# The start of a quantised feed-forward kernel: first two tiles by column block, other load queues, four part buffers

## The reference, cut to what matters

```python
scale = cond @ norm_w.T + 1.0                       # one row of 256 per sequence
ms = jnp.mean(x * x, axis=-1, keepdims=True)
h = x * (scale[:, None, :] * jax.lax.rsqrt(ms + EPS))
u = h @ up_w.T                                      # 256 -> 2048
val, gate = jnp.split(u, 2, axis=-1)
h = val * jax.nn.gelu(gate, approximate=False)      # 1024 wide
hq = act_quant(h)      # round(h * 127 / max|h|), per token
wq = weight_quant(down_w)   # -1, 0, 1 times the mean of |down_w|
y = hq @ wq.T + x                                   # 1024 -> 256
```

## Time and profile before

| | |
|---|---|
| median of three runs | 429.09 us |
| the profiled execution, own time | 429.27 us |
| its span, first to last instruction | 427.5 us |
| TensorE busy | 421.1 us (99%) |
| VectorE busy | 280.4 us (66%) |
| ScalarE busy | 186.4 us (44%) |
| GpSimd busy | 179.9 us (42%) |
| HBM read and written | 20.00 MB and 8.39 MB |

### The profile page before, as it was taken

One profiled execution on the slowest core, in us unless ns is written; L12 is line 12 of the kernel. 1 busy time (PEld: TensorE's weight loads), 2 busy tenths in 40 slices (PEclk: granted clock), 3 DMA queues, 4 the chain that ended last, 5 costly groups with the idle time before them and its releaser, 6 DMA issues.

```text
span 427.5 us, 7667 instructions
## 1 busy us (share of the span) xinstructions
PE 421.1 (99%) x2081; PEld 337.6 (79%) x2081; DVE 280.4 (66%) x539; ACT 186.4 (44%) x334; POOL 179.9 (42%) x323
## 2 busy tenths in 40 slices
PE   7999999999999999999999999999999999999997
PEld 5688888888887888887888888888878888878786
DVE  4987567556577566576565675565675665765676
ACT  5753444443444444444434444434444434444441
POOL 1564435435345344354344354353453353553520
PEclk9999999999999999999999999999999999999999
DMA  8434443334444334434244433343443344342324
GB/s 281 147 80 115 100 118 103 75 97 123 98 105 115 71 100 106 115 98 107 74 114 98 120 100 77 94 123 98 108 113 73 98 111 109 98 108 75 87 51 124
DMA packets 82024, 45.01 MB, mean 105 GB/s; under 512 B 68256, under 2 KB 68704, under 8 KB 81888
## 3 DMA queue, kind: packets, MB, share of 16 engines
q1 hardware_dynamic: 81584, 44.33, 39.8%
q10 hardware_dynamic: 432, 0.59, 0.4%
HBM read 20.00 MB, written 8.39 MB: 66 GB/s over the span
## 4 chain that ended last, share of the span: by engine, by line
PE 94%; DMA 1%; DVE 1%; SPq 1%; POOL 1%; issue 1%; ACT 0%; DVEq 0%; POOLq 0%
PE p_gate L678 41%; PE p_val L678 41%; PE p_y L698 12%; DMA up_raw<-up_w_t 1%; SPq L219 1%; DVE y_sb L500 0%; PE p_val L650 0%; POOL a_hi L311 0%; POOL scaled L308 0%; PE p_gate L650 0%; DVE q_rounded L526 0%; DVE h L547 0%; PE p_gate L657 0%; POOL a_lo L315 0%; DVE last_max L509 0%
## 5 line engine op out<-in xcount | busy, mean ns | idle before, releaser
L547 DVE SCALAR_TENSOR_TENSOR h<-p_val,rstd,gelu 128x512 f32<-128x512 f32 x128 | 95.3, 746 | 129.9 <-PE p_val L678 129.5
L389 ACT ACTIVATE gelu<-p_gate,rstd 128x512 f32<-128x512 f32 x128 | 87.5, 684 | 149.1 <-PE p_gate L678 139.4
L304 POOL TENSOR_TENSOR mean_sq_eps<-mean_sq,rms_eps 128x1 f32<-128x1 f32 x64 | 12.2, 190 | 224.3 <-PE p_val L678 210.3
L361 ACT ACTIVATE q<-q_rounded 128x1024 bf16<-128x1024 f32 x63 | 66.7, 1058 | 78.2 <-DVE q_rounded L582 78.2
L678 PE MATMUL p_gate<-up_hi,a_lo 128*128 128x512 f32 x248 | 80.6, 406 | 0.6 <-POOL a_lo L315 0.6
L678 PE MATMUL p_val<-up_hi,a_hi 128*128 128x512 f32 x248 | 78.2, 396 | 0.0
L678 PE MATMUL p_val<-up_hi,a_lo 128*128 128x512 f32 x248 | 78.1, 396 | 0.0
L678 PE MATMUL p_val<-up_lo,a_hi 128*128 128x512 f32 x248 | 78.1, 396 | 0.0
L678 PE MATMUL p_gate<-up_lo,a_hi 128*128 128x512 f32 x248 | 78.1, 395 | 0.0
L678 PE MATMUL p_gate<-up_hi,a_hi 128*128 128x512 f32 x248 | 78.1, 395 | 0.0
L568 DVE TENSOR_REDUCE h_max<-h 128x1 f32<-128x1024 f32 x63 | 76.6, 1216 | 1.2
(11 more groups left out here) (74 smaller groups left out, 247.1 us busy)
## 6 DMA issues: line engine op xcount, KB each, us to landing
xt_in<-x_t SPq DMA_DIRECT2D x32, 256.0 KB, 2.8
x_all<-x SPq DMA_DIRECT2D x32, 256.0 KB, 2.9
out<-y_sb SPq DMA_DIRECT2D x31, 256.0 KB, 2.0
up_raw<-up_w_t SPq DMA_DIRECT2D x6, 256.0 KB, 5.4
down_raw<-down_w_t SPq DMA_DIRECT2D x1, 1024.0 KB, 8.0
q_t<-q SPq DMA_TRANSPOSE x63, 3.1
up_raw<-up_w_t ACTq DMA_DIRECT2D x2, 256.0 KB, 3.1
out<-y_sb SPq DMA_DIRECT2D x1, 128.0 KB, 2.0
```

The lines of the kernel that those rows point to most:

```text
L304: pool.tensor_tensor(mean_sq_eps[:, j:j + 1], mean_sq[:, j:j + 1], rms_eps[:, :], ALU.add).then_inc(pool_step, 1)
L361: act.activation(q[j % 2][:, :], q_rounded[j % 2][:, :], ACT.Copy, bias=-ROUND).then_inc(q_ready, 1)
L389: act.activation(gelu[c][:, :], p_gate[c][:, :], ACT.Gelu, scale=rstd[:, j:j + 1]).then_inc(gelu_done, 1)
L547: nc.vector.scalar_tensor_tensor(h[s][:, c * W:(c + 1) * W], p_val[c][:, :], rstd[:, j:j + 1], gelu[c][:, :], op0=ALU.mult, op1=ALU.mult). ...
```

## The change

- The four pieces of tiles 0 and 1 run in another order: block 0 of tile 0, block 0 of tile 1, block 1 of tile 0, block 1 of tile 1 (`early_up`). Of these two tiles the gate and value of tile t go to p_gate[t] and p_val[t] instead of p_gate[c] and p_val[c]. Inside a column group of these tiles high and low products alternate.
- ScalarE and VectorE follow: up_hi and up_lo of block 1 are interleaved with the first gelu and h (`early_gelu`, `early_h`).
- All weight loads go on SyncE's queue, in the order in which they are needed, with x_t of the second sequence ahead of down_w. cond_norm alone is loaded from GpSimd's queue.
- GpSimd makes a_hi and a_lo of tile 1 (before: ScalarE and VectorE), ahead of the two rstd.
- a_hi and a_lo have four buffers. In the loop GpSimd waits for the value columns of tile t - 3 instead of t - 2.
- `ternary` has two stages, both in tile 2, and its last step, down_t, is done by ScalarE with a Copy, behind the second gelu of tile 2.
- 10 constant matmuls ahead of the scale instead of 7, on a tile of ones instead of zeros. The scale has one bank and one VectorE instruction for each k.

The diff, cut to its core (`quantised` and `rescale` are the lines L567 to L590 as functions):

```diff
-        a_lo = [sb(f"a_lo{i}", [P, KD, P], fp32r) for i in range(2)]
+        a_hi = [sb(f"a_hi{i}", [P, KD, P], fp32r) for i in range(UNIT)]
+        a_lo = [sb(f"a_lo{i}", [P, KD, P], fp32r) for i in range(UNIT)]
         squares = [sb(f"squares{i}", [P, D], fp32) for i in range(2)]
...
+            def load_up(c, k):
+                sp.dma_start(up_raw[:, c, k, :], up_w_t[c // 2, c % 2, :, k, :]).then_inc(up_in[c * KD + k], 16)
+
+            load_up(0, 0)
+            load_xt(0, 0)
+            load_up(0, 1)
+            load_up(1, 0)
+            load_up(1, 1)
+            load_x(0, 0)
+            for c in (2, 3):
                 for k in range(KD):
-                    sp.dma_start(up_raw[:, c, k, :], up_w_t[c // 2, c % 2, :, k, :]).then_inc(up_in[c * KD + k], 16)
-
-            sp.dma_start(cond_norm_sb[:, :], cond_norm).then_inc(cond_norm_in, 16)
-            load_xt(0, 0)
-            load_up(1)
-            load_up(2)
-            load_x(0, 0)
-            load_up(3)
+                    load_up(c, k)
+            load_xt(0, 1)
             sp.dma_start(down_raw[:, :, :], down_w_t).then_inc(down_in, 16)
...
                         if first and j == 1:
-                            sp.wait_ge(first_a_ready, 2)
-                        else:
-                            sp.wait_ge(a_ready, UNIT * u + j - 1)
+                            sp.wait_ge(first_a_ready, 1)
+                        sp.wait_ge(a_ready, UNIT * u + j)
...
+            pool.dma_start(cond_norm_sb[:, :], cond_norm).then_inc(cond_norm_in, 16)
...
+            pool.wait_ge(xt_landed[0], 16)
+            product(0, 1)
+            low_part(1, 5)
+            mean(0, 0)
+            root(0, 6)
+            mean(1, 1)
+            root(1, 7)
+            for j in range(TPB, UNIT):
+                if j % TPB == 0:
+                    pool.wait_ge(xt_landed[j // TPB], 16)
+                product(0, j)
+                low_part(j, BEFORE + PER_TILE * (j - 2) + 2)
+                mean(j, j)
+                root(j, BEFORE + PER_TILE * (j - 2) + 3)
+
+            with pool.Fori(1, UNITS) as u:
                 for j in range(UNIT):
-                    tile(u, j, first)
-
-            units(pool, unit)
+                    t = UNIT * u + j
+                    step = BEFORE + PER_TILE * (t - 2)
+                    if j % TPB == 0:
+
+                        pool.wait_ge(xt_landed[j // TPB], 16 * (u + 1))
+
+                    pool.wait_ge(val_done, NP * (t - 2))
+                    mean(t, j)
+                    product(u, j)
+                    low_part(j, step + 3)
+                    root(j, step + 3)
...
-            for k in range(KD):
-                act.dma_start(up_raw[:, 0, k, :], up_w_t[0, 0, :, k, :]).then_inc(up_in[k], 16)
...
-
-            for c in range(NP * 2):
+            for c in range(2):
                 for k in range(KD):
-                    act.wait_ge(up_in[c * KD + k], 16)
-                    act.activation(up_hi[:, c, k, :], up_raw[:, c, k, :], ACT.Copy).then_inc(up_hi_ready, 1)
-                if c == 2:
-                    square(0, 0, True)
-            act.wait_ge(xt_landed[0], 16)
-            act.wait_ge(scale_ready, 1)
-            for k in range(KD):
-                last = act.activation(a_hi[1][:, k, :], xt_in[0][:, k, 1, :], ACT.Copy, scale=scale_t[:, k, 0:1])
-            last.then_inc(second_a_hi_ready, 1)
+                    high_part(c, k)
+            square(0, 0, True)
+            square(0, 1, True)
+            high_part(2, 0)
+            early_gelu(0, 0)
+            high_part(2, 1)
+            high_part(3, 0)
+            high_part(3, 1)
+            early_gelu(1, 0)
+            early_gelu(0, 1)
+            act.wait_ge(down_in, 16)
+            act.activation(down_tmp[:, :, :], down_raw[:, :, :], ACT.Abs, accum_out=abs_sum[:, :]).then_inc(abs_ready, 1)
+            square(0, 2)
+            early_gelu(1, 1)
+            integers(0, 0, True)
+            square(0, 3)
...
+                    if first and j == TPB:
+
+                        act.wait_ge(ternary_step, 4)
+                        act.activation(down_t[:, :, :], down_tmp[:, :, :], ACT.Copy, bias=-ROUND).then_inc(down_ready, 1)
...
-                    nc.vector.tensor_scalar(down_tmp[:, :, :], down_tmp[:, :, :], ROUND, 1.0,
-                                            ALU.subtract, ALU.min).then_inc(ternary_step, 1)
-                if stage == 2:
-
-                    dve.wait_ge(ternary_step, 4)
-                    nc.vector.tensor_scalar(down_t[:, :, :], down_tmp[:, :, :], -1.0, None,
-                                            ALU.max).then_inc(down_ready, 1)
+                    nc.vector.tensor_scalar(down_tmp[:, :, :], down_tmp[:, :, :], ROUND + 1.0, ROUND - 1.0,
+                                            ALU.min, ALU.max).then_inc(ternary_step, 1)
...
+            for c in range(2):
+                for k in range(KD):
+                    low_part(c, k)
+            low_part(2, 0)
+            early_h(0, 0)
+            low_part(2, 1)
+            low_part(3, 0)
+            low_part(3, 1)
+            early_h(1, 0)
+            early_h(0, 1)
+            quantised(0, 0, 0)
+            early_h(1, 1)
+            quantised(0, 1, 1)
...
-                        if first and j == 1 and c == 0:
-                            ternary(1)
+                        if first and j == TPB:
+                            ternary(c)
+                        if first and j == TPB and c == 0:
+                            for done in range(TPB):
+                                rescale(0, done)
...
-            keep_busy(7)
+            keep_busy(10)
             pe.wait_ge(cond_norm_in, 16)
             for k in range(KD):
-                last = nc.tensor.matmul(p_y[0][:, k * B:(k + 1) * B], cond_norm_sb[:, B + k * P:B + (k + 1) * P],
-                                        cond_norm_sb[:, 0:B], start=True, stop=True)
-            last.then_inc(scale_done, 1)
+                nc.tensor.matmul(scale_bank[k][:, 0:B], cond_norm_sb[:, B + k * P:B + (k + 1) * P],
+                                 cond_norm_sb[:, 0:B], start=True, stop=True).then_inc(scale_done, 1)
...
+            def early_up(t, c):
+
+                n = early(t, c)
+                if t == 1 and c == 0:
+
+                    pe.wait_ge(a_ready, 1)
+                for which, bank, done, read in ((0, p_gate[t], gate_done, gelu_done), (1, p_val[t], val_done, h_done)):
+                    col = 2 * c + which
+                    if c:
+
+                        pe.wait_ge(read, n - 1)
                     for k in range(KD):
-                        if j == 0:
+                        if t == 0 and c == 0 and which == 0:
+                            pe.wait_ge(a_hi_ready, k + 1)
+                        if t == 0:
+
+                            pe.wait_ge(up_hi_ready, col * KD + k + 1)
+                        nc.tensor.matmul(bank[:, :], a_hi[t][:, k, :], up_hi[:, col, k, :], start=(k == 0), stop=False)
+                        if t == 0 and n == 0 and which == 0 and k == 0:
+                            pe.wait_ge(first_a_ready, 1)
+                        nc.tensor.matmul(bank[:, :], a_lo[t][:, k, :], up_hi[:, col, k, :], start=False, stop=False)
+                    for k in range(KD):
+                        if t == 0:
 
                             pe.wait_ge(up_lo_ready, col * KD + k + 1)
-                        last = nc.tensor.matmul(bank[:, :], a_hi[j][:, k, :], up_lo[:, col, k, :],
+                        last = nc.tensor.matmul(bank[:, :], a_hi[t][:, k, :], up_lo[:, col, k, :],
                                                 start=False, stop=(k == KD - 1))
                     last.then_inc(done, 1)
...
-                    pe.wait_ge(a_ready, t - 1)
+                    pe.wait_ge(a_ready, t)
...
             def unit(u, first, last=False):
-                for j in range(UNIT):
-                    up(u, j, 0, first)
+                for j in range(TPB if first else 0, UNIT):
+                    up(u, j, 0)
                     for n in range(downs_at(j, first, last)):
                         down(u - 1, j + n)
-                    if first and j == 1:
+                    if first and j == TPB:
 
                         pe.wait_ge(consts_ready, 1)
                         pe.wait_ge(abs_ready, 1)
                         nc.tensor.matmul(p_y[1][:, 0:1], ones[:, :], abs_sum[:, :], start=True,
                                          stop=True).then_inc(total_done, 1)
-                    up(u, j, 1, first)
-
+                    up(u, j, 1)
+
+            for c in range(NP):
+                for t in range(TPB):
+                    early_up(t, c)
```

More of the change, by code:

```diff
@@ L168, in downs_at, with early @@
             return TPB if not last else int(j == 0)
+        def early(t, c):
+            return t + TPB * c
         def y_slot(u, i):
@@ L674, in up @@
                     pe.wait_ge(read, NP * (t - 1) + c + 1)
```

(2 more changed lines are left out.)

196 lines of the change are left out of this document (85 added, 111 removed).

## The result

| | before | after |
|---|---|---|
| median (range; runs) | 429.27 us (428.94 to 431.58; 8) | 433.79 us (432.79 to 434.08; 8) |
| ratio, 95% interval | | 1.0094 (1.0079 to 1.0109) |
| profiled execution, span | 427.5 us | 431.0 us |
| first 128x512 matmul | 6.01 | 6.82 |
| A, block 0 of tile 1 starts | (another order) | 12.78 |

The changed kernel is slower by 0.94%. The profiled execution of after is the shortest of its eight, so its rows show 3.5 us of span where the medians are 4.5 us apart. Of the 3.5 us, 3.0 are there when tile 4 starts, and this stretch explains itself line by line. I read the same views as for before: the page, then the timelines of the first 35 us.

The account below looks back on a forecast made before the run. TensorE was taken to be full from tile 2 to the tail, so loop and tail cost 0; 1.45 us gained at the start is waited away at tile 4: 429.27 + 0.15 = 429.4 us, range 428.3 to 431.3.

Parts of the forecast that it names:

- Step 1: Start: cond_norm lands from GpSimd's queue at 4.2 and the first large matmul comes 1.77 us later, at 6.0.
- Step 2: Block 0 of tile 0: its 12 matmuls run from 6.01 to 10.23 as before, so A = 10.2.
- Step 3: a_lo of tile 1, now made by GpSimd, ends between 7.5 and 9.1 and is hidden.
- The slower rival: Start: VectorE making up_lo locks out GpSimd's tile 1 products; A up to 11.7, about 430.5 us, chance 0.22.
- both mechanisms: Start: VectorE and GpSimd contending (about 430.5 us, chance 0.22); cond_norm late from GpSimd's queue (430.5, chance 0.11).
- Step 4: Tiles 0 and 1: the other 36 matmuls run without a gap in 8.40 us; tile 2 at 18.6, 1.45 gained.
- Step 5: Tile 4 waits for VectorE's chain, down_t, square and GpSimd; starts at A + 21.3 = 31.5, 1.4 us behind TensorE alone.
- Step 6: Sum: tile 4 is +0.15 us against 31.35, nothing behind it is late; total 429.4 us.
- unchanged, also 0: The tail: its code is unchanged, so its cost was put at 0.

Follow-up runs that it names:

- e1: After with only cond_norm's load moved from GpSimd's queue to ScalarE's; 432.87 us, ratio to before 1.0087.
- e10: After with 14 constant matmuls instead of 10 and nothing else; 432.99 us, ratio to before 1.0082.
- e2: After with GpSimd's products for tile 1 waiting until VectorE has made a_lo of tile 0; 431.54 us, ratio to before 1.0054.
- e11: e8 with 18 constant matmuls instead of 14; 429.50 us, ratio to before 0.9988.
- e3: After with the square of tile 4 moved ahead of down_t on ScalarE; 431.80 us, ratio to before 1.0067.
- e5: Before with 10 constant matmuls of ones instead of 7 of zeros; 429.20 us, ratio to before 0.9986.
- e9: Before with 14 constant matmuls of ones instead of 7 of zeros; 429.63 us, ratio to before 0.9999.
- e8: After with cond_norm on ScalarE's queue, tile 4's square ahead of down_t, tile 1's a_hi/a_lo back on ScalarE/VectorE, 14 constant matmuls; 428.29 us, ratio to before 0.9967.
- e12: e8 unchanged, measured again in five rounds; 428.25 us, ratio to before 0.9965.

## Why the prediction was wrong, step by step

**Step 1, the first matmul at 6.0: too early by 0.8.** The 1.77 us from landing to first matmul were right (5.14 to 6.82 is 1.68). The landing was not: I took SyncE's 4.2 for GpSimd's queue, and it was 5.1. It has two parts: the load starts at 1.26 on GpSimd and at 0.74 on SyncE in before, and it takes 3.84 us to land instead of 3.45 (3.60 on ScalarE's queue in e1). Why GpSimd starts it only at 1.26 no row shows: it is the first instruction of GpSimd's own code, and where another one stands there, as in e1, that begins at 0.74. "DMA: Bandwidth & Descriptors" of the Trainium skill, section Latency and other measured facts, was in the right direction with its 0.4 us more, which is the second part here (3.84 against 3.45, though 3.49 in e10 and 4.18 in e2); in all the case shows 0.9 (0.75 between after and e1). Over the four kernels with this load on GpSimd's queue the scale starts between 4.80 and 5.49 us, over the six profiles with it on ScalarE's between 4.30 and 4.52 (e11, where the constants end later, aside).

**Step 2, block 0 as before, 4.22 us: took 5.96.** Of the excess of 1.74, 1.19 lies between the first and the second large matmul (1.89 apart; 0.70 in e2, where nothing is waited for): the wait for a_lo, of which about 0.3 is due to the alternating order (above). Another 0.4 is the clock: eight of the twelve large matmuls run at the lower level instead of six, with 0.2 us more for each. About 0.15 is left. I had kept the clock's rise where the earlier trace rows had it, in time; but it rose 3.1 us later (11.83 against 8.75), and the matmuls that ran before it had moved too.

**Step 3, "hidden": this is the step that failed.** It put a_lo of tile 1 on GpSimd at no cost to TensorE, and the products cost 1.19 us, the largest part of the 2.58 by which A is late (0.82 is step 1). I asked whether tile 1's a_lo would be in time for TensorE. It was, by 4 us (its end at 8.51 against A = 12.78). I did not ask what its three products would do to VectorE, which at that moment makes tile 0's a_lo. Work that finishes in time is still not hidden if it slows the instruction that TensorE waits for. The slower rival had the right pair of engines and the wrong sign: VectorE was to lock GpSimd out, with A at most 11.7. GpSimd began 0.17 us after VectorE and ran undisturbed. In e2, where the same products meet up_lo, both lose, 1.4 us on VectorE and 1.1 on GpSimd. The page "SBUF — State Buffer" of the Trainium skill, section Who interferes with whom, has the later one wait until the other's instruction is over. The rows of after and of e2 agree with that. The page also says that the order of issue decides who waits, so either engine can be the one, and with several instructions in a row on either side it says nothing on who comes out behind. I had read into it the side on which GpSimd waits. With both mechanisms that I had put in different rivals, and the clock, A left the range (11.7) by 1.1 us.

**Step 4, 8.40 us for the other 36 matmuls: right.** 12.78 to 21.18 is 8.40.

**Step 5, tile 4 at A + 21.3: right, A + 21.53.** VectorE's part was forecast at 10.93 us and took 10.97 (h at 18.64 to the end of down_tmp at 29.61), ScalarE's and GpSimd's at 4.58 and took 4.67 (29.64 to 34.31). That VectorE's part fits to 0.04 us is partly luck: q_rounded of tile 0 took 1.18 us instead of 0.75, beside GpSimd's scaled and a_hi for tile 3 (21.08 to 22.72), which looks like the same contention, and the other pieces were as much shorter in sum. e3 takes the stall away: 1.6 us from tile 2 to tile 4 (13.13 to 11.55), 1.3 of them in the span, since its A was later. By the forecast's own sum it takes away all that an earlier tile 2 gains. What I missed is that the x load stands right behind it, as e3 shows: issued at 25.43 and landed at 29.40 in after, it would have released the square about 2 us before down_t did.

**Step 6, the sum.** 2.58 us of a late A, 0.2 of the chain, 0.15 forecast: 2.96 at tile 4. From there 0.1 more to the first down product (2.90 against 2.80), and about 0.45 in the tail, where "unchanged, also 0" was not quite so: SyncE's last store is issued 0.34 us later against VectorE's last rows in after and in every kernel made from it (0.96 to 0.97 us behind the start of VectorE's last row; 0.63 in before, e5 and e9). No run was made to find its cause.

The range (428.3 to 431.3) had no term for this tail, nor for a clock that rises later than in the earlier trace rows.

Open are this tail, why the clock rises early in some executions of a program and late in others, whether the new order has a part in it (the nine late rises with it lie between 9.41 and 12.75, the two with the old order at 8.42 and 8.75; no run tests this), and the further 1.1 us by which most runs of after lie above its profiled one. The clock could explain them, as between e8 and e12, but this is not shown: no profile of such a run of after was taken.

## What to carry to other kernels

Where work is moved to an engine "beside" the critical one, price what it does to the critical one, not only whether the moved work is in time; let it start behind the piece that is wanted first, by a wait if need be. When an instruction moves ahead of another on its engine, look for who starts with the one that is pushed back: here a copy that was wanted 3 us later held the square with which the next unit begins. And a gain at the start is worth only what the next late thing leaves of it: the early clock gave nothing in the old order (e9), and the mended new order at the late clock (e12) reaches tile 4 0.5 us before the kernel before, has lost that again at the end, and both have a span of 427.5. New order and early clock together (e8) have 1.7 us less.
